# Layer norm of a graph network moved strip by strip into a chain of pooling layers, with the plain pooling as the chain's fifth layer

## The chip, the core and the metric

The kernel runs on one core of one Trainium2 chip. The metric is the device time of one launch in microseconds (us), the median of several runs.

## What is computed

Four small graph networks run one after the other over 6250 nodes with 128 features and 100000 edges; each ends in a residual `x = x + ...`. The change touches the seam between the second and the third:

```python
h = jnp.maximum(_layernorm(x), 0.0)
for l in range(4):                       # second network
    agg = segment_sum(h[src], dst) / max(deg, 1)
    h = h @ W_self[l] + agg @ W_neigh[l] + bias[l]      # then relu, but not after the last
x = x + h
h = jnp.maximum(_layernorm(x), 0.0)      # mean and variance over the 128 features of a node
aggregated = segment_sum(h[src], dst)    # third network: plain pooling, then small products
```

## The kernel before

Nodes lie as 49 blocks of 128 columns in three big tiles with features on the partitions: `A` holds x, `H` holds h, `B` the pooled sums. `C` holds the row of 1/degree, later the pooled edge features. A pooling is a dense product: TensorE multiplies the scaled rows of h (`hs`, 16 bit, two parts "high" and "low" that add up to full precision, nodes on partitions) with a table of edge counts in 8 bit that streams from memory.

`layer_chain` runs such poolings back to back. A **strip** is 7 blocks of nodes (896 columns, two halves in two accumulator banks). Six strips per layer are dense; the seventh (`LAST_S`) is gathered: POOL fetches rows of `hrows` by index in 21 units of 6 indirect DMAs, DVE builds one-hot matrices (L2298), PE multiplies 12 times per unit (L2183). A dense strip is 14 **pieces** of the table, with 16 and 12 matmuls in turn (L2159, 128x448); five pieces are in flight in `tbuf`, and SP loads the next when the oldest is used (L2105, L2106). Everything is written by hand, engine by engine; the pieces' numbers set where side work stands in PE's order:
- after piece 2 of a strip, `turn` makes the next layer's rows from the strip that has just ended: 7 products with the next layer's weight into banks 4 and 5 (L2215); ACT copies the high part out (L2258), DVE the low part (L2310), SP stores the rows to `hrows` (L2110). The gathered strip is turned after piece 12 of strip 5.
- after piece 12, `own_term` multiplies with the layer's own weight (L2195).
- at a strip's end DVE scales the sums out of the banks (L2333 `acc_read`), adds the own term (L2338), and ACT writes `H` (L2267). PE's next strip uses the same two banks and waits for `acc_read` (L2154).

Program order at the seam (`network`): `layer_chain` "sage" with four layers; then `layer_norm` (L921) over all of `A`, in transposed form, where averages over partitions are products with `avg` (L954), `gather` (L960) and `spread` (L976), and which also loads the pooled edge features into `C` (L939) and sets one row of it (L944); then `split_rows` (L1286 transposes `H`, L1272 and L1262 write `hs`, L1220 stores it, L1247 loads the first table pieces); then `layer_chain` "plain" with one layer, whose sums leave the banks by one scaling (L2331). Each of the four is a block of its own: all engines finish before the next begins. `update_nodes` follows.

## Time and profile before

| | us |
|---|---|
| three runs | 3234.71, 3235.70, 3237.24 |
| profiled execution, span | 3240.8 |
| "sage" chain, PE | 1209.98 to 2245.18 |
| seam: layer norm and `split_rows` | 2245.18 to 2304.58 |
| "plain" chain | 2304.58 to 2546.70 |

The span of the profiled execution, 3240.8 us, is the time that is known of it; it is 5.1 us over the median. TensorE is busy for 91% of it, VectorE for 32%, ScalarE for 23%, GpSimd for 34%. A timeline row gives the start, the length, the engine (PEld is PE's weight load, SPq a DMA issue of SP), the line, the operation with what it writes and reads, the number of instructions that were merged, and in brackets the engine's idle time before it and what ended that.

### The profile page before, as it was taken

Reading aid. Unit: us, or ns where it says so; the run is one execution under the profiler, and the core shown is the slowest. Engines: PE = TensorE matmul, PEld = TensorE weight load, DVE = VectorE, ACT = ScalarE, POOL = GpSimd, SP = SyncE. Lnnn points to the kernel's source line nnn. Section 1 sums busy time; section 2 is a strip of 40 time slices with the busy share of each in tenths; the row PEclk is TensorE's granted clock in tenths of the full one; section 3 lists DMA queues with packets and bytes.
Section 4 is the critical chain, followed back from the end, with each engine's and each line's share of the span. In section 5 each row is a group of like instructions: output and inputs, shape, how many; then the busy total and the mean of one; then the engine's idle time right before and its main releaser. Section 6 shows DMA issues by size and latency. Waiting matters only on the chain. (4 is left out here: it accounts for less than half of the span.)

```text
span 3240.8 us, 44117 instructions
## 1 busy us (share of the span) xinstructions
PE 2943.5 (91%) x18657; PEld 1740.9 (54%) x18657; DVE 1047.2 (32%) x1860; ACT 729.8 (23%) x1173; POOL 1114.7 (34%) x1012
## 2 busy tenths in 40 slices
PE   1799969997899869999999999999899877999998
PEld 1688835553444335555555555554355664555554
DVE  5899922223200261211111111113311483222122
ACT  4799912223100230000000000001100383011000
POOL 5000013330000004562562663664167101553564
PEclk6899979998999979999999999999899987999999
DMA  7133599994466226666665665664566213665665
GB/s 260 50 129 129 163 244 173 164 170 89 120 147 146 44 66 206 178 171 169 177 175 165 182 178 163 173 173 121 146 181 179 78 54 101 176 180 161 171 170 156
DMA packets 768367, 492.61 MB, mean 152 GB/s; under 512 B 362500, under 2 KB 749836, under 8 KB 767568
## 3 DMA queue, kind: packets, MB, share of 16 engines
q1 hardware_dynamic: 705362, 395.76, 50.5%
q0 software_dynamic: 30112, 62.69, 6.6%
q10 hardware_dynamic: 32702, 31.44, 3.1%
q8 instruction: 140, 2.29, 0.3%
q14 instruction: 51, 0.42, 0.0%
HBM read 334.89 MB, written 76.82 MB: 127 GB/s over the span
## 5 line engine op out<-in xcount | busy, mean ns | idle before, releaser
L2159 PE MATMUL acc<-tbuf,hs 128*128 128x448 fp8e4 x8232 | 1602.0, 354 | 20.0 <-PEq L1242 8.8
L2136 POOL DMA_INDIRECT grow<-hrows,glist x882 | 940.6, 1066 | 791.9 <-PE acc L2183 388.3
L2159 PEld LDWEIGHTS acc<-tbuf,hs 128*128 128x128 f16 x8232 | 801.2, 98 | 762.9 <-issue 52.5
L2298 DVE TENSOR_TENSOR edge_loc<-iota,gdl 128x768 f16<-128x768 bf16 x147 | 140.6, 971 | 743.9 <-PE acc L2183 714.4
L731 PE MATMUL quad<-K,S 128*128 128x196 bf16 x1568 | 278.0, 250 | 17.6 <-DVE K L655 17.6
L1627 PE MATMUL acc<-tbuf,hs 128*128 128x512 fp8e4 (+1 forms) x1300 | 279.6, 369 | 14.9 <-DMA tbuf<-table 14.9
L711 ACT ACTIVATE stage<-quad 128x784 fp8e4<-128x784 f32 x392 | 287.4, 838 | 11.6 <-PE quad L731 5.8
L735 PE MATMUL deg<-K,S 128*128 128x196 bf16 x1568 | 276.8, 248 | 0.0
L1500 PE MATMUL acc<-tbuf,hs 128*128 128x512 fp8e4 (+1 forms) x1300 | 267.4, 369 | 0.7 <-issue 0.7
L2267 ACT ACTIVATE H<-B,vectors 128x448 f32<-128x448 f32 (+2 forms) x56 | 37.4, 668 | 820.3 <-DVE B L2338 820.3
L1500 PEld LDWEIGHTS acc<-tbuf,hs 128*128 128x128 f16 x1300 | 123.6, 98 | 144.4 <-issue 4.3
L1627 PEld LDWEIGHTS acc<-tbuf,hs 128*128 128x128 f16 x1300 | 119.9, 98 | 139.5 <-issue 17.7
L655 DVE TENSOR_TENSOR K<-iota,win_key 128x2744 bf16<-128x2744 bf16 x112 | 177.1, 1581 | 0.0
L2333 DVE SCALAR_TENSOR_TENSOR B<-acc,scales,C 128x448 f32<-128x448 f32 (+1 forms) x84 | 57.2, 681 | 366.4 <-PE acc L2159 268.7
L731 PEld LDWEIGHTS quad<-K,S 128*128 128x128 bf16 x1568 | 152.2, 97 | 40.5 <-DVE K L655 40.2
L735 PEld LDWEIGHTS deg<-K,S 128*128 128x128 bf16 x1568 | 154.4, 98 | 0.2
L1083 POOL DMA_INDIRECT glist<-edge_pairs,gof x7 | 7.0, 1000 | 357.9 <-SPq L1067 356.0
L1645 DVE TENSOR_TENSOR Z<-iota,edge_loc 128x1024 bf16<-128x1024 bf16 x98 | 73.6, 770 | 170.2 <-PE acc L1609 123.0
L655 DVE TENSOR_TENSOR S<-iota,win_low 128x1792 bf16<-128x1792 bf16 x112 | 122.0, 1089 | 13.6 <-PEq L271 3.5
L2183 PEld LDWEIGHTS acc<-edge_loc,grow 128*128 128x128 f16 x1764 | 110.9, 98 | 24.5
L2183 PE MATMUL acc<-edge_loc,grow 128*128 128x128 f16 x1764 | 122.5, 219 | 0.0
L2125 POOL MEMSET grow<- 128x3072 f16 x3 | 8.0, 2660 | 317.3 <-POOLq L2457 163.7
(301 smaller groups left out, 2008.5 us busy)
## 6 DMA issues: line engine op xcount, KB each, us to landing
tbuf<-table SPq DMA_DIRECT2D x294, 448.0 KB, 3.6
tbuf<-table SPq DMA_DIRECT2D x294, 336.0 KB, 3.2
table<-stage SPq DMA_DIRECT2D x6, 5488.0 KB, 19.4
grow<-hrows,glist POOLq DMA_INDIRECT x882
hrows<-hs SPq DMA_DIRECT2D x28, 448.0 KB, 4.4
feat<-in_edge_attr_dram ACTq DMA_DIRECT2D x27, 448.0 KB, 6.6
C<-factors ACTq DMA_DIRECT2D x2, 3136.0 KB, 12.5
table<-stage SPq DMA_DIRECT2D x2, 2744.0 KB, 12.2
```

The source lines that it names most:

```text
L655: return V.tensor_tensor(to.rearrange("p n (c t) -> p n c t", t=2), iota.rearrange("p (c t) -> p c t", t=2).unsqueeze(1).to_broadcast([P, ...
L711: A.activation(stage[:, b, :, to:to + 4 * WD].rearrange("p b (w d) -> p w b d", d=WD), pair[(h * NQUAD + q) % 3][:, :].rearrange("p (t c) ...
L731: mm = T.matmul(pair[quad % 3][:, at:at + NKEY], S[:, q, i, :], K[:, q, i, :], start=(w % 2 == 0), stop=True, skip_group_check=True)
L735: mm = T.matmul(deg[:, w % 2 * NKEY:(w % 2 + 1) * NKEY], S[:, q, i, :], K[:, q, i, :], start=(w == 0), stop=(u == NHALF * NBATCH - 1 and i ...
L1500: mm = nc.tensor.matmul(acc[h][:, 0:n * P], k.hs[:, j, part, :], counts[:, :, j // 2, :, j % 2], start=(j == 0 and part == 0), stop=(j == ...
L1627: mm = T.matmul(acc[g % 2][:, 0:n * P], k.hs[:, j, part, :], counts[:, :, j // 2, :, j % 2], start=(j == 0 and part == 0), stop=(j == NL - ...
L1645: V.tensor_tensor(Z[:, u % 2, :, :].rearrange("p n (c t) -> p n c t", t=2), k.iota[:, 0:EWIN].rearrange("p (c t) -> p c t", t=2).unsqueeze ...
L2136: g.indirect_dma_start(out=grow[:, n % 2, t, :], out_offset=None, in_=k.hrows[l % 2], in_offset=bass.IndirectOffsetOnAxis(k.glist[:, i // ...
L2159: mm = T.matmul(acc(s, h), rows[l % 2][:, g * US + r, part, :], counts[:, (r - lo) * STRIP + h * HALF:(r - lo) * STRIP + (h + 1) * HALF], ...
L2183: mm = T.matmul(to, grow[:, n % 2, t, part * P:(part + 1) * P], hot[:, n % 2, t, :], start=(not conv and i % GU == 0 and t == 0 and part = ...
L2298: V.tensor_tensor(hot[:, n % 2, :, :], k.iota[:, 0:P].unsqueeze(1).to_broadcast([P, GH, P]), k.gdl[:, i // GU, i % GU * GH:(i % GU + 1) * ...
L2333: V.scalar_tensor_tensor(dst[:, at], acc(s, q), scale(1, l), k.C[:, at], ALU.mult, ALU.mult).then_inc(acc_read.h, 1)
```

## The change

- The chain "sage" gets a fifth layer (`l == LO`), the plain pooling, with scale 0 and neither weight nor own term. `layer_norm`, `split_rows` and the chain "plain" are no longer called there.
- In the fourth layer (`norm`), DVE adds each finished strip plus its bias to `A` (`residual`) where ACT wrote `H`. After piece 2 of the next strip PE transposes the 7 blocks of `A` into banks 4 and 5 (`turn`); DVE takes mean and variance per block there (`moments`), ACT the root, DVE the reciprocal; ACT scales, shifts and clips the 7 blocks into `ny` (`spread`) and writes the high parts, DVE the low parts (`rests`). After piece 8 PE transposes `ny` back (`turn_back`), and ACT copies that to `H` (`back`). The gathered strip is turned after piece 12 of strip 5 and goes back after piece 2 of the fifth layer; strip 5 is turned after piece 3 there.
- The row stores of that layer stand five pieces later in SP's order. The load of `C` stands between table pieces in strip 1 of the fifth layer, the row of ones ahead of that layer's gathers on POOL.
- In every chain PE's wait ahead of a layer's first piece is for strip 4's low parts, no longer for the gathered strip's.

```diff
+BACK_AT, NORM_STORE = 8, 7
...
-    L = len(layers)
+    LO = len(layers)
+    sage, conv = kind == "sage", kind == "conv"
+    L = LO + 1 if sage else LO
     R = k.ring
     total, turns = L * DENSE * NH, (L - 1) * NU
-    sage, conv = kind == "sage", kind == "conv"
+    norm = LO - 1 if sage else None
...
-        return k.scales[:, part, at_scale + l:at_scale + l + 1]
+        at = at_scale + l if l < LO else 0
+        return k.scales[:, part, at:at + 1]
...
+        if sage:
+            ny = k.rstd[:, :, :].rearrange("p a c -> p (a c)")
...
-                        stores[piece + R + 2] = (l, s)
+                        stores[piece + R + (NORM_STORE if l == norm else 2)] = (l, s)
                 for n in range(R, total):
                     sp.wait_ge(used.h, used.at(n - R + 1))
                     load_piece(k, sp, tbuf, n // NH % DENSE, n % NH, n % R)
...
                         l, s = stores[n]
                         sp.wait_ge(z_lo.h, z_lo.at(2 * turned[l, s] + 2))
                         store_rows(k, sp, rows[(l + 1) % 2], (l + 1) % 2, s * US, (s + 1) * US)
+                    if sage and n == LO * DENSE * NH + 2 * NH:
+                        sp.wait_ge(acc_read.h, acc_read.at(count(norm, DENSE - 1, 1)))
+                        sp.dma_start(edges[0:3 * DE, :], k.ea_sums[0:3 * DE, ELEFT:ELEFT + NP]
+                                     ).then_inc(k.sem("easum_in").h, 16)
...
+                    if l == LO:
+                        pool.wait_ge(acc_read.h, acc_read.at(count(norm, DENSE - 1, 1)))
+                        g.memset(edges[3 * DE:3 * DE + 1, :], 1.0)
...
-                        if leaves and j > turns:
+                        if l == norm and normed(l, s):
+                            pe.wait_ge(n_H.h, n_H.at(2 * (normed(l, s) - 1) + q + 1))
+                        elif leaves and j > turns:
...
+                            elif l == norm:
+                                mm = T.transpose(to, k.A[:, b * P:(b + 1) * P], k.idf[:, :])
...
+                def turn_back(l, s):
+                    for q in range(2):
+                        pe.wait_ge(n_y.h, n_y.at(2 * normed(l, s) + q + 1))
+                        for i, b in enumerate(blocks_of(s, q)):
+                            mm = T.transpose(k.bank[4 + q][:, i * P:(i + 1) * P],
+                                             ny[:, (HALVES[q][0] + i) * P:(HALVES[q][0] + i + 1) * P], k.idf[:, :])
+                        mm.then_inc(n_back.h, 1)
...
-                                pe.wait_ge(z_lo.h, z_lo.at(2 * (turned[l - 1, DENSE - 1] - 1) + 2))
+                                pe.wait_ge(z_lo.h, z_lo.at(2 * (turned[l - 1, DENSE - 1] - 2) + 2))
...
-                            if i == TURN_AT:
+                            if i == TURN_AT and sage and l == LO and s == 0:
+                                turn_back(norm, LAST_S)
+                            if i == (TURN_AT + 1 if sage and l == LO and s == 0 else TURN_AT):
                                 for e in events(l, s)[0:1]:
                                     if e[1] != LAST_S:
                                         turn(*e)
-                            if i == OWN_AT and sage:
+                            if i == BACK_AT and events(l, s) and events(l, s)[0][0] == norm:
+                                turn_back(*events(l, s)[0])
+                            if i == OWN_AT and sage and l < LO:
...
+                def spread(l, s):
+                    n = normed(l, s)
+                    act.wait_ge(n_mv.h, n_mv.at(n + 1))
+                    A.activation(nrs[:, :], nmv[:, :, 1], ACT.Sqrt, bias=k.eps[:, 0:1]).then_inc(n_std.h, 1)
+                    act.wait_ge(n_rs.h, n_rs.at(n + 1))
+                    for q in range(2):
+                        lo, hi = HALVES[q]
+                        for i in range(lo, hi):
+                            ins = A.activation(ny[:, i * P:(i + 1) * P], k.bank[4 + q][:, (i - lo) * P:(i - lo + 1) * P],
+                                               ACT.Relu, scale=nrs[:, i:i + 1], bias=nsh[:, i:i + 1])
+                        ins.then_inc(n_y.h, 1)
+                    for q in range(2):
+                        lo, hi = HALVES[q]
+                        act.wait_ge(n_y.h, n_y.at(2 * n + q + 1))
+                        A.activation(rows[(l + 1) % 2][:, s * US + lo:s * US + hi, 0, :],
+                                     ny[:, lo * P:hi * P].rearrange("p (a f) -> p a f", f=P), ACT.Copy,
+                                     scale=scale(0, l + 1)).then_inc(z_hi.h, 1)
+                def back(l, s):
+                    for q in range(2):
+                        b = blocks_of(s, q)
+                        act.wait_ge(n_back.h, n_back.at(2 * normed(l, s) + q + 1))
+                        A.activation(v[:, b[0] * P:(b[-1] + 1) * P], turn_bank(q, len(b)), ACT.Copy).then_inc(n_H.h, 1)
...
-                    if sage:
+                    if sage and l < norm:
...
+                        if sage and l == LO and s == 0:
+                            back(norm, LAST_S)
...
+                def residual(l, s, q):
+                    at = chunk_of(s, q)
+                    dve.wait_ge(moved.h, moved.at(count(l, s, q)))
+                    V.scalar_tensor_tensor(k.A[:, at], dst[:, at], layers[l][3], k.A[:, at], ALU.add, ALU.add
+                                           ).then_inc(ready.h, 1)
+                def moments(l, s):
+                    for q in range(2):
+                        lo, hi = HALVES[q]
+                        dve.wait_ge(z_full.h, z_full.at(2 * turned[l, s] + q + 1))
+                        for i in range(lo, hi):
+                            ins = V.bn_stats(nst[:, i, :], k.bank[4 + q][:, (i - lo) * P:(i - lo + 1) * P])
+                    link(ins)
+                    for i in range(US):
+                        ins = V.bn_aggr(nmv[:, i, :], nst[:, i, :])
+                    ins.then_inc(n_mv.h, 1)
+                    dve.wait_ge(n_std.h, n_std.at(normed(l, s) + 1))
+                    link(V.reciprocal(nrs[:, :], nrs[:, :]))
+                    V.scalar_tensor_tensor(nsh[:, :], nmv[:, :, 0], -1.0, nrs[:, :], ALU.mult, ALU.mult
+                                           ).then_inc(n_rs.h, 1)
+                def rests(l, s):
+                    j = turned[l, s]
+                    for q in range(2):
+                        lo, hi = HALVES[q]
+                        to = rows[(l + 1) % 2][:, s * US + lo:s * US + hi, :, :]
+                        dve.wait_ge(z_hi.h, z_hi.at(2 * j + q + 1))
+                        V.scalar_tensor_tensor(to[:, :, 1, :], ny[:, lo * P:hi * P].rearrange("p (a f) -> p a f", f=P),
+                                               scale(0, l + 1), to[:, :, 0, :], ALU.mult, ALU.subtract
+                                               ).then_inc(z_lo.h, 1)
...
-                    if not sage and not conv:
+                    if not conv and l >= LO - (0 if sage else 1):
...
+                        mine = units(s)[2:] + units(s + 1)[:2]
+                        if sage and l == LO and s == 0:
+                            rests(norm, LAST_S)
                         for e in events(l, s)[0:1]:
-                            if e[1] != LAST_S:
+                            if e[0] == norm:
+                                moments(*e)
+                                for h in mine[:1]:
+                                    hots(l, h)
+                                mine = mine[1:]
+                                rests(*e)
+                            else:
                                 turned_in(*e)
-                        for h in units(s)[2:] + units(s + 1)[:2]:
+                        for h in mine:
                             hots(l, h)
                         parts = [(s, 0), (s, 1)]
+                            if l == norm:
+                                residual(l, LAST_S, 0)
...
                         if s == DENSE - 1:
                             leave_bank(l, LAST_S, 1)
                             if conv:
                                 finish(l, LAST_S, 1)
-                            turned_in(l, LAST_S)
+                            if l == norm:
+                                residual(l, LAST_S, 1)
+                                moments(l, LAST_S)
+                            else:
+                                turned_in(l, LAST_S)
                         for c in parts:
                             leave_bank(l, *c)
+                        for c in parts if l == norm else ():
+                            residual(l, *c)
...
-        k.rstd = sb("rstd", [NCH, 2, CH], F32)
+        k.rstd = sb("rstd", [P, 2, CH], F32)
...
-                layer_chain(k, "sage", H, B, layers, 2, tbuf, factor=1)
+                layer_chain(k, "sage", H, B, layers, 2, tbuf, factor=1, edges=C)
...
-        layer_norm(k, A, H, B, add=True, edges=C)
-        with table_buffer(k, True) as tbuf:
-            split_rows(k, H, True, 0, None, None, tbuf, False, not spilled)
-            if spilled:
+        if spilled:
+            layer_norm(k, A, H, B, add=True, edges=C)
+            with table_buffer(k, True) as tbuf:
+                split_rows(k, H, True, 0, None, None, tbuf, False)
                 pool_neighbours(k, B, None, None, tbuf, False, H, None, 0)
-            else:
-                layer_chain(k, "plain", H, B, [()], 0, tbuf)
```

TensorE at the seam, before (L960 and L976 are the layer norm's averages, L1286 the 49 transposes of `H`, L2159 the plain chain's dense products, L2183 its first gathered unit):

```order
L954 MATMUL acc<-A,avg 128x448
L960 MATMUL acc<-B,gather 7x448 x8
L976 MATMUL acc<-parts,spread 128x448 x14
L935 UNCONDITIONAL_BRANCH
L1276 UNCONDITIONAL_BRANCH
L1286 MATMUL acc<-idf,H 128x128 x49
L1242 UNCONDITIONAL_BRANCH
L2140 UNCONDITIONAL_BRANCH
L2159 MATMUL acc<-tbuf,hs 128x448 x224
L2183 MATMUL acc<-edge_loc,grow 128x128 x12
```

TensorE there now (L2180 dense, L2204 gathered, L2216 own terms, L2238 `turn`, L2248 `turn_back`; the fourth layer ends 12 matmuls into the row of 56):

```order
L2204 MATMUL acc<-edge_loc,grow 128x128 x12
L2216 MATMUL acc<-H,weights 128x384
L2180 MATMUL acc<-tbuf,hs 128x448 x28
L2216 MATMUL acc<-H,weights 128x448 x2
L2238 MATMUL acc<-idf,A 128x128 x7
L2180 MATMUL acc<-tbuf,hs 128x448 x56
L2248 MATMUL acc<-idf,rstd 128x128 x7
L2180 MATMUL acc<-tbuf,hs 128x448 x12
L2238 MATMUL acc<-idf,A 128x128 x7
L2180 MATMUL acc<-tbuf,hs 128x448 x72
L2248 MATMUL acc<-idf,rstd 128x128 x7
L2180 MATMUL acc<-tbuf,hs 128x448 x96
```

The averages are gone, and the transposes stand in groups of 7 between dense products, with no branch to another block. The other five pairs of groups stand in the fourth layer's strips 1 to 5.

VectorE at the end of the fourth layer, before:

```order
L2298 TENSOR_TENSOR edge_loc<-iota,gdl 128x768 x2
L2333 SCALAR_TENSOR_TENSOR B<-acc,scales,C 128x384
L2338 TENSOR_TENSOR B<-B,acc 128x384
L2333 SCALAR_TENSOR_TENSOR B<-acc,scales,C 128x448
L2338 TENSOR_TENSOR B<-B,acc 128x448
L2333 SCALAR_TENSOR_TENSOR B<-acc,scales,C 128x448
L2338 TENSOR_TENSOR B<-B,acc 128x448
L2095 UNCONDITIONAL_BRANCH
```

and now (L2444 and L2449 are the two operations that were L2333 and L2338; L2383 is `residual`, L2409 `rests`):

```order
L2444 SCALAR_TENSOR_TENSOR B<-acc,scales,C 128x384
L2449 TENSOR_TENSOR B<-B,acc 128x384
L2383 SCALAR_TENSOR_TENSOR A<-B,vectors,A 128x384
L2392 BN_STATS nst<-acc 128x6 x7
L2395 BN_AGGR nmv<-nst 128x2 x7
L2398 RECIPROCAL nrs<-nrs 128x7
L2399 SCALAR_TENSOR_TENSOR nsh<-nmv,nrs 128x7
L2444 SCALAR_TENSOR_TENSOR B<-acc,scales,C 128x448
L2449 TENSOR_TENSOR B<-B,acc 128x448
```

The moments of the gathered strip now stand ahead of the operation that frees the first bank for the fifth layer.

SP's queue around the load of `C`, before and now:

```order
L1175 DMA tbuf<-table 128x3x448
L2095 UNCONDITIONAL_BRANCH
L937 UNCONDITIONAL_BRANCH
L939 DMA C<-ea_sums 96x6272
L935 UNCONDITIONAL_BRANCH
```

```order
L1175 DMA tbuf<-table 128x3x448
L1175 DMA tbuf<-table 128x4x448
L2127 DMA C<-ea_sums 96x6272
L1175 DMA tbuf<-table 128x3x448
L1175 DMA tbuf<-table 128x4x448
```

It moved from the idle seam to a place between two table pieces.

## Rows read from the trace of the kernel before

**Rows 1.** Page: busy time and share of the span, by engine.
```profile
PE 2943.5 (91%) x18657; PEld 1740.9 (54%) x18657; DVE 1047.2 (32%) x1860; ACT 729.8 (23%) x1173; POOL 1114.7 (34%) x1012
```

**Rows 2.** Timeline: PE at the end of the chain "sage" (us: start, length).
```profile
2242.75 2.43 PE L2159 MATMUL acc<-tbuf,hs 128*128 128x448 fp8e4 x12
```

**Rows 3.** Timeline: the start of the chain "plain", and DVE at its strip 0's end.
```profile
2304.58 45.35 PE L2159 MATMUL acc<-tbuf,hs 128*128 128x448 fp8e4 x224 [5.74 <-PEq L1242]
...
2343.54 0.68 DVE L2331 TENSOR_SCALAR B<-acc,scales 128x448 f32<-128x448 f32 x1 [37.04 <-PE acc L2159]
```

**Rows 4.** Windows: stretch, busy time by engine, PE's granted clock, DMA share, GB/s.
```profile
2245.18:2304.58 59.40, 40.35 (x120) 14.86 (x120) 42.68 (x66) 20.68 (x35) 5.32 (x1) 0.85 0.43 115
...
2305.00:2315.00 10.00, 10.00 (x41) 4.57 (x40) 1.50 (x2) 0.00 (x0) 5.96 (x5) 0.73 0.52 144
```

**Rows 5.** Chain that ended last, second network after: pieces (start, us, what).
```profile
3020.74 3.03 PE acc L2159 x16
3023.77 0.77 PE acc L2213 x7
3024.53 5.30 PE acc L2159 x28
3029.83 0.67 PE acc L2183 x12
```

**Rows 6.** Timeline: "sage" layer 1, PE and DVE at the ends of strip 5 and strip 0.
```profile
1474.38 8.08 PEld L2159 LDWEIGHTS acc<-tbuf,hs 128*128 128x128 f16 x44 [0.24 <-issue]
...
1482.74 1.73 PE L2215 MATMUL acc<-weights,H 128*128 128x128 f32 x14
...
1510.78 1.67 PE L2195 MATMUL acc<-H,weights 128*128 128x448 f32 x4
...
1513.62 0.68 DVE L2333 SCALAR_TENSOR_TENSOR B<-acc,scales,C 128x448 f32<-128x448 f32 x1 [26.06 <-PE acc L2159]
```

**Rows 7.** Timeline of `update_nodes`: statistics on DVE, then scaling on ACT.
```profile
2552.58 0.86 DVE L2660 BATCH_NORM_STATS2 st_u<-u 128x6 f32<-128x128 f32 x4
...
2558.59 1.65 ACT L2563 ACTIVATE u<-u,sh_u,rs_u 128x128 f32<-128x128 f32 x4 [3.91 <-DVE sh_u L2682]
```

**Rows 8.** Single lines of `update_nodes`: count, duration ns min/median/max.
```profile
L2665 DVE BATCH_NORM_AGGREGATE mv_u<-st_u x196: 147/149/184, 2553.5 to 2701.0; 128x2 f32<-128x6 f32 x196
...
L2571 ACT ACTIVATE rs_u<-mv_u,eps x19: 296/299/308, 2553.9 to 2708.7; 128x16 f32<-128x16 f32 x19
```

**Rows 9.** Waits of PE in "sage": who waited for whom, us, times, longest.
```profile
PE acc L2159 <- DVE B L2333: 6.9, 4, 1.7
...
PE acc L2159 <- DMA tbuf<-table: 2.5, 1, 2.5
```

**Rows 10.** Timeline: a 3136 KB load on ACT's queue beside the table pieces, strip 0.
```profile
1225.48 0.42 ACTq L2275 DMA_DIRECT2D C<-factors  x1
...
1238.51 0.13 PEld L2159 LDWEIGHTS acc<-tbuf,hs 128*128 128x128 f16 x2 [2.91 <-DMA tbuf<-table]
...
1241.85 8.67 PEld L2159 LDWEIGHTS acc<-tbuf,hs 128*128 128x128 f16 x46 [0.22 <-issue]
```

**Rows 11.** DMA issues: size and us to landing; alone, then in 2651:2668, usual.
```profile
C<-ea_sums SPq DMA_DIRECT2D x1, 2352.0 KB, 13.2
...
C<-factors SPq DMA_DIRECT2D x1, 3136.0 KB, 11.3
hrows<-hs SPq DMA_DIRECT2D x1, 1024.0 KB, 14.0
...
tbuf<-table SPq DMA_DIRECT2D x294, 336.0 KB, 3.2
```

**Rows 12.** Timeline: last row store for layer 1, and its first gathers.
```profile
1490.20 0.49 SPq L1220 DMA_DIRECT2D hrows<-hs  x1
...
1494.71 0.99 POOL L2136 DMA_INDIRECT grow<-hrows,glist  x1 [40.33 <-DMA hrows<-hs]
1496.01 1.00 POOL L2136 DMA_INDIRECT grow<-hrows,glist  x1 [0.30 <-issue]
```

27 lines of the change are left out of this document (22 added, 5 removed).

## The prediction

> **What bounds the kernel now.** I read the page first. TensorE is busy for 91% of the span and VectorE for 32% [rows 1], so what counts is where PE doesn't pool. Then I read the timeline at the two chains' borders: PE's last dense product of "sage" ends at 2242.75 + 2.43 = 2245.18 [rows 2], its first of "plain" starts at 2304.58 [rows 3]. The seam between them lasts 59.4 us, in which PE is "busy" for 40 us [rows 4], but with averages and transposes that wait for DVE and ACT: nothing of it is pooling. In a chain, PE is filled with dense products and has hardly any waits: 6.9 us for the banks and 2.5 us for the table in all four layers [rows 9]. So a stage that is hidden there costs only its own instructions on PE.
>
> **What is removed.** The whole seam: -59.4 us on PE's path. With it goes the slow start of "plain". Its strip 0 needs 2343.54 - 2304.58 = 39.0 us until DVE may leave the first bank [rows 3]. The same stretch in layer 1 of "sage" needs 1513.62 - 1474.38 = 39.2 us, of which one turn (1.6) and the own terms (1.5) fall away in a plain layer [rows 6]: 36.1. The difference is 2.8 us, and the window from 2305 shows why, a clock at 0.73 for 10 us, between the levels of 1.2 and 2.4 GHz, 2.7 us lost [rows 4]. If PE never stops, this is saved too: -2.8. The rest of the plain layer, 241 us, stays as it is.
>
> **What is added on PE.** 14 groups of 7 transposes (7 strips, there and back). A group of 7 transposes of this kind, in the midst of dense products, takes 0.77 us on the chain of waits, where 16 dense matmuls take 3.03 and 28 take 5.30 [rows 5]. 14 x 0.77 = +10.8. I take it for exact; if half the groups cost as much as a turn with weights (1.6 us [rows 6]), it would be 16.6, the upper bound.
>
> **Does the norm of a strip hide?** From the end of a turn, T: statistics of 7 blocks at 0.215 each (0.86 for 4 [rows 7]) 1.5, which start while the turn ends, so T+1.4; 7 aggregates at 0.147, 1.0; root 0.30 [rows 8]; reciprocal and product on as small tiles, taken at the root's price, 0.6; for four hand-overs I add 0.4. That gives T+3.7. ACT's 7 blocks at 1.65 / 4 = 0.41 [rows 7] take 2.9: `ny` is full at T+6.6. High and low parts, two operations on each engine of 0.6 to 0.7 us, end at about T+9. PE comes to `turn_back` after 6 pieces in strips 1 to 5 (84 matmuls, 15.9 us) and after 5 in the last (13.6 us). It needs the last strip's rows at piece 10, 14.4 us after that turn. The cover is 14 against 7, and 14 against 9: no wait. The statistics here read the banks and not SBUF, which no row shows; even at double their price they end 2.5 us later and stay hidden. Without that cover each microsecond beyond it would be paid 7 times.
>
> **One place where it doesn't hide.** The gathered strip is turned after piece 12 of strip 5, and its moments stand on DVE ahead of the operation that frees bank 0. The queue behind the wait for ACT's root is DVE's own: `leave_bank` (5,0), and behind that PE, which wants the bank for the fifth layer one piece after T, at T+2.3 (12 matmuls). DVE gets to it at T+3.7 and needs 0.68 [rows 6]: T+4.4. Stall: +2.0, once; bounds 1.3 and 3.0. Two waits of 1.7 us for the same banks are known from before [rows 9]. The low parts' wait ahead of a layer's first piece, which now is looser, costs nothing before (PE goes on after 0.24 us [rows 6]); 0.
>
> **The later row stores.** They stand five pieces later, and the fifth layer's gathers wait for the last one. From that layer's start: 10 pieces 26.5, three groups 2.3, SP's issue 0.6: 29.4. From issue to the first gather 4.5 us [rows 12], then six gathers 1.3 apart [rows 12]: the last ends at 41.4. PE wants the first unit after 16 pieces, 224 matmuls 42.4 + 2.3 = 44.7. Three us are left for the last gather to land, which no row shows by itself. +0.5, bounds 0 and 2. The row of ones (a POOL instruction of 5.3 us [rows 4]) ends long before and is hidden by the same wait.
>
> **The load of `C`.** This is the DMA that was moved, from an idle seam to a busy queue. Alone it lands after 13.2 us [rows 11]. Behind it on SP's queue stand table pieces, of which PE has 5 in hand: 72 matmuls and one gathered unit, 14.3 us. Does a piece behind it wait? In `update_nodes` a row store that is issued 0.4 us after a 3136 KB load on this same queue lands after 14.0 us, 3 us after the load is through [rows 11]. So yes. At that store's pace (1024 KB in 3 us) the piece ahead of the load takes 1.3 us; the piece behind it 1.0 by that pace, or its usual 3.2. It lands at 13.2 + 1.3 + 1.0 to 3.2 = 15.5 to 17.7, and PE waits 1.2 to 3.4 us. The other case is the load of 3136 KB on ACT's queue beside the pieces: PE waited 2.5 us [rows 9, 10]. Both meet at +2.5, which I take; bounds 0 (gaps in the load used by the pieces) and 6 (the gathers take a share as well). After that earlier wait PE's weight loads of 0.15 us stand with 0.22 us between them, 0.37 us for each, instead of 0.19, from 1238.5 to 1241.85 [rows 10]: the clock's lower level, for 9 matmuls, 1.7 us. After waits of 1.7 us no such row follows. I add +1.7 for this stall, and nothing for the one of 2.0.
> Trainium skill, page "DMA: Bandwidth & Descriptors", section "Queues, rings and completion order": on each DMA engine the descriptors of one ring are taken in order, and the engine goes round between the queues that have work. This speaks against the new place: by the rule, pieces of another queue would share with the load, and those behind it in SP's ring can't. The trace agrees with the first part in the pieces beside ACT's load, and with the second in the store of 14.0 us; the rule alone would put the stall at the upper end, 3.4, 0.9 us above my value.
>
> **Sum.** -59.4 - 2.8 + 10.8 + 2.0 + 0.5 + 2.5 + 1.7 = -44.7. The profiled execution becomes 3240.8 - 44.7 = 3196.1. It stood 5.1 us above the median of 3235.7; taken off the median, **3191.0 us**.
>
> **Rivals.**
> 1. *The load of `C` hides after all* and the clock stays up: -4.2, so 3186.8. For it: the DMA engines are only half busy at such a place [rows 4]. Against it: the store of 14.0 us. 20%.
> 2. *The norm's chain is longer than its cover, or the small operations get in the way of others* (one-hot matrices that DVE builds late for gathers, statistics from the banks): 2 us in each of the 7 strips is +14, 3205.0. For it: DVE's order has three new places where it waits. Against it: 14 us of cover for 7 to 9 us of work. 13%.
> 3. *The chain doesn't close*: at the border PE waits for something that I have not seen, and half of the seam comes back as idle time (30 us): 3221.0. For it: five engines' queues, each in strict order, must fit together. Against it: the order shows dense products on both sides of the border, and the waits point to work that is long done. 3%.
> 4. *Slower than before.* The place is `turn_back`: PE stands in its strict order in front of it until ACT has filled `ny`. If a strip's norm took x us, each strip would cost x - 15.9 us (13.6 in the last). It decides from (44.7 / 7) + 15.6 = 22 us per strip; at 24 us the kernel would need 3191.0 + 7 x 8.4 = 3249.8. The rows for the parts add up to a third of that, so 2%.
> 5. *The sum is too careful*: no stall at all, neither for the bank, the gather or the table: -51.4, so 3184.3. 7%.
>
> **How the numbers follow.** The forecast's own case, all terms within their bounds, 3187 to 3199, holds 55%. Rivals 1 and 5 below it and most of rival 2 above are taken in with 3184 to 3206. The bounds' ends together (transposes 16.6, bank 3.0, gather 2, load 6 and two falls of the clock 3.4) give -31.2, 3204.5; the lower ends (1.3, 0, 0) give -50.1, 3185.6. What the range leaves out, rivals 3 and 4, part of rival 2 and mishaps outside all cases, is 10 to 15%. A measurement of this kernel can tell 0.2%, 6.5 us, from no change; nearly all cases are far below that. Faster 0.95, same 0.02, slower 0.03.
>
> **What will show it.** The fourth layer's last dense product and the fifth's first should be 2 us apart, with the wait on DVE's `B`, not 59. A group of 7 transposes should add 0.8 us. DVE's `BATCH_NORM` rows should take 0.2 to 0.3 us and ACT's root follow within 4 us of a turn; `turn_back` should show no wait. One wait of PE for `tbuf` should stand in strip 2 of the fifth layer, 2 to 3 us long, with weight loads 0.37 us apart behind it; none there means rival 1. A wait of PE for `grow` in strip 1 of that layer speaks on the gather term. Waits before transposes in every strip would mean rival 2 or 4. The prediction fails as a whole if the time around the seam was not PE's alone, so that work after it (`update_nodes`, the last chain) becomes longer in turn.

## The result, and the profile after

| | before | changed |
|---|---|---|
| median, us | 3236.5 (3234.7 to 3244.9) | **3194.2** (3187.7 to 3200.5) |
| ratio | 1 | 0.9869, 95% interval 0.9855 to 0.9883 |
| the same two kernels measured again | 3236.6 (3233.6 to 3242.1) | 3190.7 (3189.0 to 3192.7); ratio 0.9859 (0.9844 to 0.9874) |
| span of the profiled execution | 3240.8 | 3192.1 |

The change brings 42 us in the first comparison and 46 in the second. The forecast was 44.7 less, 3191.0 us. The two traces lie 48.7 us apart; the table below shows which part of that belongs to the change.

The page of the changed kernel, busy time by engine. It answers to [rows 1]: TensorE is busy 33 us less, and still for 91% of the span.

```profile
PE 2910.6 (91%) x18636; PEld 1733.9 (54%) x18636; DVE 1040.9 (33%) x1937; ACT 737.7 (23%) x1210; POOL 1108.2 (35%) x1011
```

The timeline of PE around the old seam: start and length in us, line, operation, count, and in brackets the idle time ahead of it with what ended it. L2238 is the turn there, L2248 the turn back.

```profile
2246.79 0.93 PE L2238 MATMUL acc<-idf,A 128*128 128x128 f32 x7
2247.55 2.43 PE L2180 MATMUL acc<-tbuf,hs 128*128 128x448 fp8e4 x12
2251.04 8.48 PE L2180 MATMUL acc<-tbuf,hs 128*128 128x448 fp8e4 x44 [1.05 <-DVE B L2444]
2259.36 0.93 PE L2248 MATMUL acc<-idf,rstd 128*128 128x128 f32 x7
2260.12 2.43 PE L2180 MATMUL acc<-tbuf,hs 128*128 128x448 fp8e4 x12
2262.39 0.93 PE L2238 MATMUL acc<-idf,A 128*128 128x128 f32 x7
2263.16 13.78 PE L2180 MATMUL acc<-tbuf,hs 128*128 128x448 fp8e4 x72
2276.78 0.93 PE L2248 MATMUL acc<-idf,rstd 128*128 128x128 f32 x7
2277.54 18.32 PE L2180 MATMUL acc<-tbuf,hs 128*128 128x448 fp8e4 x96
```

Where 59.4 us lay between two dense products [rows 2, 3], one wait of 1.05 us is left. The 12 products ahead of it are the fourth layer's last piece; the fifth layer begins with the 44 behind it. The dense products go on 0.76 to 0.77 us after the start of each group of transposes, and no group waits.

What VectorE and ScalarE do in the same stretch, one strip's norm:

```profile
2247.43 1.49 DVE L2392 BATCH_NORM_STATS2 nst<-acc 128x6 f32<-128x128 f32 x7 [5.96 <-PE acc L2238]
2248.95 0.58 DVE L2395 BATCH_NORM_AGGREGATE nmv<-nst 128x2 f32<-128x6 f32 x7
2249.56 0.30 ACT L2293 ACTIVATE nrs<-nmv,eps 128x7 f32<-128x7 f32 x1 [15.38 <-DVE nmv L2395]
2249.89 0.20 DVE L2398 RECIPROCAL nrs<-nrs 128x7 f32<-128x7 f32 x1 [0.37 <-ACT nrs L2293]
2250.13 0.17 DVE L2399 SCALAR_TENSOR_TENSOR nsh<-nmv,nrs 128x7 f32<-128x7 f32 x1
2250.21 0.68 DVE L2444 SCALAR_TENSOR_TENSOR B<-acc,scales,C 128x448 f32<-128x448 f32 x1
2250.33 2.55 ACT L2298 ACTIVATE rstd<-acc,nsh,nrs 128x128 f32<-128x128 f32 x7 [0.47 <-DVE nsh L2399]
...
2253.90 1.27 DVE L2409 SCALAR_TENSOR_TENSOR hs<-rstd,scales,hs 128x512 f16<-128x512 f32 x2
```

The waits of PE in the chain of five layers (whole time, how often, the longest); they answer to [rows 9]:

```profile
PE acc L2180 <- DVE B L2444: 8.0, 5, 1.7
PE acc L2180 <- DMA tbuf<-table: 7.3, 2, 4.4
```

One more wait for a bank (the 1.05), and a second one for a table slot: the 4.4 us, at the place of the load of `C`. The issue on SP's queue, PE's first dense product behind the wait, and its weight loads at the lower clock, 0.37 us apart:

```profile
2319.50 0.50 SPq L2127 DMA_DIRECT2D C<-ea_sums  x1
2322.12 19.88 SPq L1175 DMA_DIRECT2D tbuf<-table  x6
...
2337.77 3.82 PE L2180 MATMUL acc<-tbuf,hs 128*128 128x448 fp8e4 x12 [4.42 <-DMA tbuf<-table]
...
2338.12 0.15 PEld L2180 LDWEIGHTS acc<-tbuf,hs 128*128 128x128 f16 x1 [0.22 <-issue]
2338.49 0.15 PEld L2180 LDWEIGHTS acc<-tbuf,hs 128*128 128x128 f16 x1 [0.22 <-issue]
```

The DMA issues of 2319 to 2342 (KB, us to landing); [rows 11] had 13.2 for the same load alone:

```profile
C<-ea_sums SPq DMA_DIRECT2D x1, 2352.0 KB, 16.1
```

**Where the time went.** I cut both traces at three places of PE: the first dense product of the chain, its first gathered unit, and the first product of `update_nodes`.

| us | before | changed | difference |
|---|---|---|---|
| up to the first dense product | 1210.0 | 1209.4 | -0.6 |
| to the first gathered unit | 49.9 | 46.9 | -3.0 |
| to `update_nodes` (**"the stretch"** from here on) | 1287.2 | 1242.7 | **-44.5** |
| to the end | 693.8 | 693.2 | -0.6 |

The -3.0 belong to no edit. They are the clock of the first 128 dense products, 24.37 us at the upper level and 26.06 where it starts late, and of the 56 behind the first layer's wait (10.77 or up to 12.45), less 0.4 for that wait's own length. Over the kernels below whose first layer is the same, that stage lies between 46.9 and 50.1 us and follows this clock and the length of that wait (2.48 to 3.65 us): before 49.9, e6 (before's chain) 48.9, e1 and e5 (the changed chain) 50.0 and 50.1. The last row moves without an edit too: the changed kernel traced a second time (e8) has 690.2 us there, and all thirteen traces lie between 690.0 and 694.0. So the stretch, in which the unchanged kernel repeats to 0.1 us, is what I compare below.

### The profile page after: what moved, and what is told of

Its sections match the earlier page's. It is cut to its first block and busy times, and to the rows that moved or that the text cites. A ratio compares the mean times of both kernels' runs of the same rounds, so it can differ in the third digit from the quotient of the medians.

```text
span 3192.1 us, 44150 instructions
## 1 busy us (share of the span) xinstructions
PE 2910.6 (91%) x18636; PEld 1733.9 (54%) x18636; DVE 1040.9 (33%) x1937; ACT 737.7 (23%) x1210; POOL 1108.2 (35%) x1011
## 5 line engine op out<-in xcount | busy, mean ns | idle before, releaser
L2180 PE MATMUL acc<-tbuf,hs 128*128 128x448 fp8e4 x8232 | 1599.5, 353 | 20.0 <-DVE B L2444 8.0
L2180 PEld LDWEIGHTS acc<-tbuf,hs 128*128 128x128 f16 x8232 | 799.7, 98 | 757.7 <-issue 42.2
L731 PE MATMUL quad<-K,S 128*128 128x196 bf16 x1568 | 277.7, 250 | 15.9 <-DVE K L655 12.5
L2444 DVE SCALAR_TENSOR_TENSOR B<-acc,scales,C 128x448 f32<-128x448 f32 (+1 forms) x84 | 57.2, 681 | 357.3 <-PE acc L2180 259.9
L2336 ACT ACTIVATE H<-B,vectors 128x448 f32<-128x448 f32 (+2 forms) x42 | 28.1, 668 | 584.3 <-DVE B L2449 584.3
L2204 PEld LDWEIGHTS acc<-edge_loc,grow 128*128 128x128 f16 x1764 | 110.9, 98 | 24.4
L2204 PE MATMUL acc<-edge_loc,grow 128*128 128x128 f16 x1764 | 122.5, 219 | 0.0
L2339 ACT ACTIVATE B<-B,vectors 128x448 f32<-128x448 f32 (+2 forms) x28 | 18.7, 668 | 421.9 <-DVE H L2452 421.7
```

The lines of the kernel that those rows point to most:

```text
L731: mm = T.matmul(pair[quad % 3][:, at:at + NKEY], S[:, q, i, :], K[:, q, i, :], start=(w % 2 == 0), stop=True, skip_group_check=True)
L2180: mm = T.matmul(acc(s, h), rows[l % 2][:, g * US + r, part, :], counts[:, (r - lo) * STRIP + h * HALF:(r - lo) * STRIP + (h + 1) * HALF], ...
L2204: mm = T.matmul(to, grow[:, n % 2, t, part * P:(part + 1) * P], hot[:, n % 2, t, :], start=(not conv and i % GU == 0 and t == 0 and part = ...
L2444: V.scalar_tensor_tensor(dst[:, at], acc(s, q), scale(1, l), k.C[:, at], ALU.mult, ALU.mult).then_inc(acc_read.h, 1)
```

## The experiments

Unless something else is said, each is the changed kernel with one edit. e1 to e6, e9 and e10 are one launch each, the traced one, so their total times say little beside a difference of a few microseconds; what counts is the stretch. "Stage" in the recorded texts is mostly the time from the chain's first dense product, that is the stretch and the first layer's 46.9 to 50.1 us with its changing clock; I judge them by the stretch.

### What does the load of `C` cost, and why?

Theory: pieces behind it on SP's queue have to wait for their turn. Rival: it is the amount of data at once. **e1** has it on ACT's queue.

```diff
-if sage and n == LO * DENSE * NH + 2 * NH:                     # SP
-    sp.wait_ge(acc_read.h, ...); sp.dma_start(edges[0:3 * DE, :], ...)
+if sage and l == LO and s == 1:                                # ACT
+    act.wait_ge(used.h, used.at(LO * DENSE * NH + 2 * NH - R + 1))
+    act.wait_ge(acc_read.h, ...); act.dma_start(edges[0:3 * DE, :], ...)
```

> The same 2352 KB load of C at the same moment, but issued on ACT's queue instead of SP's. In the changed kernel PE waits 4.4 us for a table piece there, and 1.4 us more go to the lower clock behind it. Theory (order in the queue): pieces no longer stand behind the load, so the wait falls to 0 to 2.5 us (the 3136 KB load on ACT's queue costs 2.5 to 2.8 us in the first layer), and PE's time from the first dense product of the chain to the first product of update_nodes falls by 2 to 5.8 us. Rival (bandwidth alone: the DMA engines have the same bytes to move): the wait stays at 4 us, the stage is unchanged within 1 us.

Measured: 3197.6 us; the stretch 1245.2, 2.6 longer. The wait did not go, it grew, and came one piece earlier; neither the theory nor the rival had it longer. Timeline of PE, and the DMA queues in the midst of the load, in 2326:2334 (packets, MB, share of the 16 engines; q10 is ACT's, q1 SP's):

```profile
2340.23 7.34 PE L2176 MATMUL acc<-tbuf,hs 128*128 128x448 fp8e4 x28 [6.51 <-DMA tbuf<-table]
```
```profile
q10 hardware_dynamic: 69, 1.73, 96.7%
q1 hardware_dynamic: 70, 0.06, 4.1%
```

The load moves 69 packets of 25 KB there, one per row, and the table 70 of 0.9 KB: one for one. So the load has 96.7% of the engines' time and the pieces 4.1%, the pieces that were ahead of it on SP's queue among them. The Trainium skill, page "DMA: Bandwidth & Descriptors", section "Queues, rings and completion order", says that an engine changes queues at packet granularity, taking a whole packet from one ring before the next. The trace agrees with these counts; I had used the rule without asking for the size of a turn.

In the changed kernel, with the load on SP's queue, the same stretch of the load (2323:2332) reads:

```profile
DMA packets 131, 2.13 MB, mean 236 GB/s; under 512 B 20, under 2 KB 20, under 8 KB 51
q1 hardware_dynamic: 79, 1.98, 98.5%
```

The 79 packets of SP's queue hold 25 KB each on average, rows of the load, and none in the whole stretch has the size of the table's 0.9 KB (as many are under 2 KB as under 512 B): for 9 us the pieces behind the load get nothing. So the order within the queue is how the wait comes about there, as the theory had it. What e1 refutes is that leaving this queue helps: sharing packet by packet with rows of 25 KB left the pieces hardly more than nothing, and the wait began one piece earlier.

**e5** cuts the load into seven parts of 896 columns on SP's queue, one every 7 pieces, and `update_nodes` waits for all seven.

```diff
-if sage and n == LO * DENSE * NH + 2 * NH:
-    sp.dma_start(edges[0:3 * DE, :], k.ea_sums[0:3 * DE, ELEFT:ELEFT + NP]).then_inc(...)
+part = n - LO * DENSE * NH - 2 * NH
+if sage and part >= 0 and part % 7 == 0 and part // 7 < EDGE_PARTS:
+    at = part // 7 * STRIP
+    sp.dma_start(edges[0:3 * DE, at:at + STRIP],
+                 k.ea_sums[0:3 * DE, ELEFT + at:ELEFT + at + STRIP]).then_inc(...)
```

> The load of C stays on SP's queue, in 7 parts of 336 KB (896 columns each), one behind every seventh table piece from the same place on. Theory (a piece behind the load waits for the whole load): a part delays the pieces by some 2 us, less than the 14 us that PE has in hand, so PE waits for no piece and the clock stays up: stage -5.8 us against the changed kernel. Rival (the bytes beside the table stream are what costs): the 4.4 us come back in small waits, stage unchanged within 1 us.

Measured: 3189.2 us; the stretch 1236.7, 6.0 shorter, as the theory said. PE has no wait for the table in the fifth layer. The parts, in 2310:2490:

```profile
C<-ea_sums SPq DMA_DIRECT2D x7, 336.0 KB, 4.8
```

So the load costs 5.8 to 6.0 us in the changed kernel: 4.42 of wait, and 1.4 because 12 products took 3.82 us instead of 2.43.

Parts differ from the one load in two ways: pieces go between them, and their rows are short. **e9** issues all seven at once on SP's queue, **e10** all seven at once on ACT's.

```diff
 if sage and n == LO * DENSE * NH + 2 * NH:                     # e9: SP; e10: at e1's place, ACT
-    sp.dma_start(edges[0:3 * DE, :], ...)
+    for at in range(0, NP, STRIP):
+        sp.dma_start(edges[0:3 * DE, at:at + STRIP], ...)
```

> The changed kernel, with the load of C cut into the seven parts of 896 columns as in e5, but all seven issued one behind the other at the place of the one load, on SP's queue. It tells the length of a row (12.5 KB of padded columns before, 3.5 KB now) from the amount that is ahead of the table's next piece. Theory A (what counts on this queue is the 2352 KB ahead of the next piece; the parts of e5 helped because the pieces went between them): PE's wait for a table slot in strip 2 of the fifth layer stays, 3.5 to 5 us, and the stretch from the first gathered unit to update_nodes stays at 1242 to 1244 us. Theory B (long rows move badly, short ones don't): the wait falls below 1 us and the stretch is 1236 to 1238 us, as in e5.

> The same seven parts, all issued one behind the other at the same moment on ACT's queue. e1 had the one load there: the wait was 6.5 us and one piece earlier, against 4.4 on SP's queue. Theory C (the two queues take turns packet by packet, so the load's 22 KB packets take most of the engines' time against the table's of under 2 KB): with packets of 3.5 KB the table keeps a third or more of the engines' time, about 90 of the 180 GB/s that PE uses; over the 14 us of the load it falls some 7 us of work behind, which the full slots nearly cover (the 13.4 us of work that e0's load displaces became a wait of 4.4, so they cover about 9). Expected wait 0 to 1.5 us, stretch 1236 to 1239 us. Theory D (the amount at once decides, whatever the row): wait 4.4 to 6.5 us, stretch 1242 to 1246 us.

("e0's load" in the second text is the one of the changed kernel. The first text gives a row of the one load as 12.5 KB; it is 24.5 KB, 2352 KB over 96 rows.) Measured: e9 3190.0 us, e10 3195.9. The wait in each, and the queues of e10 in 2334:2338:

```profile
2335.61 3.84 PE L2183 MATMUL acc<-tbuf,hs 128*128 128x448 fp8e4 x12 [2.93 <-DMA tbuf<-table]
```
```profile
2342.52 3.95 PE L2177 MATMUL acc<-tbuf,hs 128*128 128x448 fp8e4 x12 [4.27 <-DMA tbuf<-table]
```
```profile
q10 hardware_dynamic: 216, 0.67, 62.2%
q1 hardware_dynamic: 215, 0.19, 21.0%
```

| 2352 KB | SP's queue: wait, stretch | ACT's queue: wait, stretch |
|---|---|---|
| at once, long rows | 4.42, 1242.7 | 6.51, 1245.2 |
| at once, seven parts | 2.93, 1241.5 | 4.27, 1242.7 |
| spread over 42 pieces | none, 1236.7 | not run |

The one load was traced at its place in five kernels, with waits of 4.3 to 4.7 us, so the differences in the table are clear of that. My theory C for e10 (0 to 1.5 us) fell, and so did B for e9 (below 1 us): short rows take 2.2 us off the wait on ACT's queue and 1.5 on SP's, but the amount at once keeps the larger part. A (3.5 to 5 us) and D (4.4 to 6.5) were nearer, and both a little too high. In this part of e10 the queues again move packets one for one (216 and 215), with 3.1 KB in one of the load's on average: it has 62.2% of the time, and the table 21.0%, not the third that C wanted. On SP's queue there are no such turns, and part of the gain must be another: by the rows of 2323:2332 the long rows take 98.5% of 9 us for 1.98 MB, and e9's short ones in 2323:2331 86.0% of 8 us for 1.73 MB:

```profile
q1 hardware_dynamic: 564, 1.73, 86.0%
```

That is an estimate of 10.8 us of all engines for the whole load in long rows and 9.6 in short ones, 1.2 of the 1.5 us. No run takes the two effects apart on ACT's queue.

The windows of the changed kernel compare the load with what the engines have left (stretch, busy time by engine, clock, DMA share, GB/s):

```profile
2265.00:2300.00 35.00, 35.00 (x199) 18.82 (x197) 5.83 (x11) 4.94 (x12) 11.16 (x11) 1.00 0.68 188
...
2319.00:2330.00 11.00, 11.00 (x69) 5.95 (x66) 1.64 (x2) 0.00 (x0) 8.52 (x9) 1.00 1.00 244
2330.00:2340.00 10.00, 5.58 (x25) 2.46 (x24) 0.68 (x1) 0.00 (x0) 2.00 (x2) 0.86 0.99 268
```

The layer itself uses 188 GB/s at a DMA share of 0.68; with the load the engines are full at 244 to 268. That leaves 56 to 80 GB/s, and 2.41 MB in 16 us want 150. Whatever the order, PE's pieces lose the rest, which at 188 GB/s is 6 to 8 us of work; the full slots cover a part of it, and 4.4 are seen. In e5 the parts are issued over 119 us, so that the load wants 20 GB/s, and each lands after 4.8 us, less than the 14 us of pieces that PE has in hand. The budget is an account from these rows; what the runs show is that spreading cures the wait and that neither another queue nor short rows alone does.

### Does DVE's place for the moments cost the bank wait?

**e2** puts the moments of the gathered strip behind the operations that free the banks.

```diff
 if l == norm:
     residual(l, LAST_S, 1)
-    moments(l, LAST_S)
 ...
 for c in parts:
     leave_bank(l, *c)
+if l == norm and s == DENSE - 1:
+    moments(l, LAST_S)
```

> The moments of the gathered strip stand behind the operations that free the two banks on DVE, not ahead of them. Theory: PE's wait of 1.05 us ahead of the fifth layer's first product goes (0 to 0.2 us), and the norm of that strip, some 3 us later, is still covered by the pieces ahead of turn_back: stage -1.0 us. Rival: what PE waits for there is something else that ends at the same time, or turn_back now waits as long: stage unchanged.

Measured: 3188.2 us; the stretch 1241.7, 0.9 shorter, as the theory had it. In PE's timeline dense product follows dense product, and the turn back 10.6 us later still waits for nothing:

```profile
2244.04 0.93 PE L2238 MATMUL acc<-idf,A 128*128 128x128 f32 x7
2244.81 10.76 PE L2180 MATMUL acc<-tbuf,hs 128*128 128x448 fp8e4 x56
2255.40 0.93 PE L2248 MATMUL acc<-idf,rstd 128*128 128x128 f32 x7
```

### What is the looser wait for the low parts worth?

In the changed kernel PE waits ahead of a layer's first piece for one strip fewer than before. I had put that at 0. **e3** takes the wait back to what it was.

```diff
-... turned[l - 1, DENSE - 1] - 2) + 2
+... turned[l - 1, DENSE - 1] - 1) + 2
```

> PE's wait ahead of a layer's first piece is for the gathered strip's low parts again, as in the kernel before. Theory: in the fifth layer these end at T+7.6 after the strip's turn, 5.4 us after PE gets there, so the wait grows from 1.05 to 5.4 us and the clock falls behind it: stage +4.3 to +6.0 us; at the starts of layers 2, 3 and 4 nothing changes (0.2 us at most). Rival: other waits come anyway within those 5 us (turn_back, the bank), so that it costs less than 2 us.

Measured: 3200.3 us; the stretch 1250.2, 7.5 longer, above the range of the text. Timeline of PE at the border:

```profile
2256.67 10.86 PE L2180 MATMUL acc<-tbuf,hs 128*128 128x448 fp8e4 x44 [5.25 <-DVE hs L2409]
```

The wait costs 4.2 more than the one of 1.05; behind it 44 products take 10.86 us instead of 8.48 (2.4). These 6.6 us lie at the border. The other 0.9 lie at the load of `C` (a wait 0.25 longer, products behind it 0.7), where traces without this edit differ by 0.3 (e2, e8), so that it is not shown whether they belong to it. Layers 2 to 4 start as before, without a new wait. So the edit is worth nothing where it stood, and 6.6 to 7.5 us once the norm's chain ends at the border.

### How long may a strip's norm be?

**e4** gives ACT four passes instead of one over each strip's 7 blocks, 7.7 us more per strip.

```diff
+for r in range(3):                                             # pad is ny
+    for q in range(2):
+        lo, hi = HALVES[q]
+        for i in range(lo, hi):
+            ins = A.activation(pad[:, i * P:(i + 1) * P], k.bank[4 + q][...], ACT.Relu, scale=nrs[...], bias=nsh[...])
+    ...                                                        # ACT waits for its own pass
 for q in range(2):                                             # the pass that counts, as before
```

> ACT scales and clips the 7 blocks of a strip four times instead of once, the first three for nothing, one after the other: each strip's norm is 7.8 us longer. Theory (cover of 13.6 to 15.9 us per strip, of which 5.3 are used): only the gathered strip's turn_back (11.8 us after its turn, n_y now at 13.1) and the last strip's rows (needed 14.4 us after the turn, there after 15) become late: +1 to +4 us in all. Rival (each microsecond of a strip's norm counts in every strip): +30 to +55 us.

Measured: 3191.2 us; the stretch 1245.0, 2.3 longer. Timeline of ACT and PE (L2181 is the dense product there, L2249 the turn back):

```profile
2247.40 7.73 ACT L2300 ACTIVATE rstd<-acc,nsh,nrs 128x128 f32<-128x128 f32 x21 [0.47 <-DVE nsh L2408]
...
2257.77 0.55 PE L2249 MATMUL acc<-idf,rstd 128*128 128x128 f32 x3 [0.39 <-ACT rstd L2307]
2258.15 2.43 PE L2181 MATMUL acc<-tbuf,hs 128*128 128x448 fp8e4 x12
...
2274.81 0.93 PE L2249 MATMUL acc<-idf,rstd 128*128 128x128 f32 x7
```

54 us more of ACT's work cost PE 1 us, all at the gathered strip, whose cover is the shortest (11.8 us). The other 1.4 lie at the load of `C`: its wait is 4.72 instead of 4.42, and the 12 products and the gathered unit behind it take 1.1 longer. The edit doesn't touch that place, and it is not shown why. The last strip's rows, which the text expected late too, cost no wait. The other six strips hide 13 us of norm (5.3 + 7.7 until `ny` is full) whole. So the length of a strip's norm, on which rivals 2 and 4 rest, was far from costing anything.

### Is the slow start of "plain" the clock?

**e6** is the kernel *before*, with 42 products into an unused bank at the end of the seam, whose results nobody reads.

```diff
+if store and weight is None:
+    for _ in range(42):
+        nc.tensor.matmul(k.bank[6][:, 0:2 * P], k.idb[:, :], k.iota[:, 0:2 * P], start=True, stop=True)
```

> The kernel before with 42 products of 128x256 into an unused bank at the end of split_rows ahead of the chain plain, whose results nobody reads: PE is busy while SP's stores finish, instead of idle for 5.7 us. Theory (the plain chain starts at the lower clock because PE was idle): strip 0 of that chain, from its first product to DVE's first operation on the bank, takes 36.2 us instead of 39.0, the granted clock in its first 10 us is near 1.0 instead of 0.73, and the stage is 2.8 us shorter. Rival (the slow start is the table's first pieces or the start of the block): it stays at 38 to 39 us. The seam is not shortened in either case; if the products outlast the stores it is longer by up to 1 us.

Measured: 3234.6 us; the stretch 1284.3, 2.9 shorter than before's.

```profile
2296.09 4.75 PE L1292 MATMUL acc<-iota,idb 128*128 128x256 bf16 x42
2302.25 42.53 PE L2162 MATMUL acc<-tbuf,hs 128*128 128x448 fp8e4 x224 [1.41 <-PEq L1242]
...
2338.39 0.68 DVE L2334 TENSOR_SCALAR B<-acc,scales 128x448 f32<-128x448 f32 x1 [34.22 <-PE acc L2162]
```
```profile
2300.00:2310.00 10.00, 8.59 (x49) 4.54 (x48) 1.83 (x2) 0.00 (x0) 5.38 (x4) 1.00 0.77 215
```

From the first product to DVE's operation 2338.39 - 2302.25 = 36.1 us, against 39.0 [rows 3], and a clock of 1.00 where it was 0.73 [rows 4]. The seam is as long as it was (59.3 us against 59.4), so what became shorter is this strip: the term of -2.8 is the clock.

### The pieces together

**e7** is e5 and e2 in one, launched five times.

> The changed kernel with both repairs: C in 7 parts, and the moments of the gathered strip behind the operations that free the banks. Theory: the two waits and the lower clock go, 1.05 + 4.4 + 1.4 = 6.9 us less than the changed kernel, stage 1282.7 us; ratio to the kernel before 0.985. Rival (new waits take their place): stage 1287 or more, ratio as for the changed kernel, 0.987.

Measured: 3185.7 us (3184.7 to 3188.0), ratio to before 0.9844 (0.9831 to 0.9857). The stretch is 1235.5, 7.2 shorter than the changed kernel's; with the first layer it is 1282.5 us, where the text had 1282.7.

**e8** is the changed kernel again, beside e7 on the same chip.

> The changed kernel once more, beside the repaired one on the same chip: ratio to the kernel before 0.9869 within its interval of 0.9855 to 0.9883; stage from the chain's first dense product to update_nodes 1289.6 us, or up to 3 us more where the first layer starts at the lower clock as it does in the kernel before.

Measured: 3190.7 us, ratio 0.9859, the stretch 1242.6, the same as in the first trace. The medians of e7 and e8 lie 5.0 us apart, the stretches of their traces 7.1. The parts and the moments are all that differs; the medians also hold what moves without an edit (up to the first gathered unit and behind the chain).

**e11** adds one edit to e7: the first layer's load of `C<-factors` (3136 KB on ACT's queue, behind which PE waited 2.5 us in before [rows 9]) in seven parts on SP's queue, one every 7 pieces. DVE waits strip by strip for what it needs.

```diff
-act.dma_start(k.C[:, :], k.factors[factor:factor + 1, :].to_broadcast([P, NP])).then_inc(row_in.h, 16)
+if factor is not None and n >= R and (n - R) % 7 == 0 and (n - R) // 7 < EDGE_PARTS:   # SP
+    at = (n - R) // 7 * STRIP
+    sp.dma_start(k.C[:, at:at + STRIP], k.factors[factor:factor + 1, at:at + STRIP]...).then_inc(row_in.h, 16)
-dve.wait_ge(row_in.h, row_in.at(16))
+if factor is not None and l == 0 and s < 4:
+    dve.wait_ge(row_in.h, row_in.at(16 * min(2 * s + 2, EDGE_PARTS)))
```

> e7 (the load of C in parts, the moments behind leave_bank) and besides the first layer's load of C<-factors, 3136 KB in one on ACT's queue, cut into seven parts of 448 KB on SP's queue, one every 7 pieces, with DVE waiting for those it needs strip by strip instead of for all. In e7 PE waited 2.94 us for a table slot behind that load, and the matmuls behind it ran at the lower clock for some microseconds. If the cause is the same as for C: that wait falls to below 0.5 us, the stretch from the first dense product to the first gathered unit goes from 47.0 to 43 to 44 us, the rest stays at 1235.4 and the time is 3181.5 us (3180 to 3184). If the first layer's wait has another cause (the stores of hrows and the gathers that lie in the same stretch): the wait stays over 2 us and the time is 3184 to 3187.

Measured: 3182.2 us (3177.9 to 3187.6), ratio to before 0.9838 (0.9825 to 0.9852). The first 184 dense products stand without a gap:

```profile
1208.36 34.97 PE L2190 MATMUL acc<-tbuf,hs 128*128 128x448 fp8e4 x184 [2.93 <-PEq L1242]
```

From the first dense product to the first gathered unit it is 43.9 us instead of 47.0, and the rest 1235.5 as in e7. The trace shows the 3.1 us; the medians of e7 and e11 lie 3.5 apart, but their ranges overlap, and they were taken on two chips. The edit changes the queue and cuts the load at once, so it doesn't say which of the two helps here. It is the best version that was run: 54 us less than before.

## Why the prediction was right

Its -44.7 is the stretch, which became 44.5 shorter; the medians' differences of 42.3 and 45.9 us lie on both sides of it. Term by term:

| term | predicted | measured | by |
|---|---|---|---|
| seam | -59.4 | -59.4 | nothing of it is left but the waits below |
| slow start of "plain" | -2.8 | -2.8 | e6 |
| 14 groups of transposes | +10.8 | +10.8 | 0.77 between the starts, in every group |
| bank | +2.0 | +1.05 | 0.9 by e2 |
| first gather | +0.5 | 0 | no wait for `grow` |
| load of `C` | +4.2 | +5.8 | 6.0 by e5 |
| sum | -44.7 | -44.55 | |

**The bank.** The mechanism was right (e2), the size was not. DVE was at `leave_bank` 2.7 us after the turn and not 3.7. The aggregates over 7 blocks take 0.58 us from the first's start to the last's end and not 1.0, since I took the 0.147 of a single one in `update_nodes` [rows 8] for the pace, and their records overlap. The four hand-overs are in the rows' gaps, 0.1 to 0.4 us. ACT's seven blocks took 2.55 against 2.9, so `ny` was full 5.3 us after the turn against 6.6: the room under the cover was larger than told, as e4 then showed. No lower clock followed the 1.05, as assumed.

**The first gather.** The last row store was issued at 2280.41 and the first gather began 5.1 us later, not 4.5, yet PE had the first unit without a wait:

```profile
2280.41 0.51 SPq L1220 DMA_DIRECT2D hrows<-hs  x1
...
2285.49 1.00 POOL L2157 DMA_INDIRECT grow<-hrows,glist  x1 [27.97 <-DMA hrows<-hs]
...
2295.70 0.83 PE L2204 MATMUL acc<-edge_loc,grow 128*128 128x128 f16 x12
```

**The load of `C`.** The place and the kind of wait were right, and so was the step "does a piece behind it wait? so yes": for 9 us SP's queue moved nothing but the load. Wrong was what stood beside it, that on another queue the pieces would share and so fare better: they share packet by packet, which left them 4.1% and made the wait 2.1 us longer (e1). By size: the load landed after 16.1 us where I had 13.2 + 1.3, and the cover was 13.85 and not 14.3. Table packets ahead of the load still moved more than 2 us after its issue, and the gathers were at work beside it; no run takes these two apart. It was 18.3 until the piece behind it was there, beyond my upper 17.7, and the wait of 4.4 was beyond my 3.4, though within the bounds of 0 to 6 that I took. The clock's part was 1.4 for 1.7 predicted. Too small here and too large at the bank and the gather: the sum's 0.15 us of error is luck, each term missed by up to 1.6.

**What the sum did not hold** is the looser wait. It was priced at nothing because the same wait cost nothing in the kernel before. For the time predicted that is right, since the edit is in; as a price of the edit it is wrong by 6.6 to 7.5 us (e3). Without it the kernel would have come out that much later, and the change would have looked worse for a reason that no row of before shows.

**The rivals.** 1 and 5 (the load hides) fell with the 4.4 us. 2, 3 and 4 did not occur, and e4 shows how far away 2 and 4 were, as far as they rest on the length of the norm: with 7.7 us more per strip they were still not reached. The tail behind the chain did not grow: it lies between 690.0 and 694.0 us in the eleven traces with a fifth layer, and is 693.8 and 691.1 in the two of the chain before (before and e6). So the seam's time was PE's alone, to within these 4 us.

## What to carry to other kernels

A stage that sits between two chains on the bounding engine costs its whole length; laid strip by strip into the chain it costs only its own instructions there, and how much slack it has is best measured by making it longer on purpose. When a large transfer is moved into a busy stretch, compare what it wants per microsecond with what the engines have left; another queue made it worse here and short rows helped a little, but cutting it and spreading the parts took the wait away. A wait that costs nothing today must be priced again at the place where the change makes another chain end.

## What the hardware showed

- **A gap of 2.4 to 3.7 us on PE ended at the lower clock in some traces and not in others.** Behind the first layer's wait for the table 56 products took 10.77 us in six of the traces (waits of 2.84 to 3.37) and 12.24 to 12.45 in the six others (waits of 2.48 to 3.65), whatever the kernel. Two rows with the same wait:

```profile
1236.59 10.77 PE L2180 MATMUL acc<-tbuf,hs 128*128 128x448 fp8e4 x56 [2.84 <-DMA tbuf<-table]
```
```profile
1238.52 12.24 PE L2176 MATMUL acc<-tbuf,hs 128*128 128x448 fp8e4 x56 [2.84 <-DMA tbuf<-table]
```

  The first is the changed kernel, the second e1. Behind the wait of 1.05 it did not fall (44 products in 8.48 us); behind all eight of 4.3 to 6.5 it did, for 1.4 to 2.5 us, and in e9 behind one of 2.93 as well. What PE did before has a part in it: the chain's first 128 products took 26.06 us in the four traces in which PE had been idle for 3.07 to 3.13 us ahead of them, and 24.37 in the eight with 2.38 to 2.97; those four all fell again behind the wait that followed, of the eight others only two did. So a term such as my +1.7, taken from one wait of 2.5 us, was not certain; it held because the wait became 4.4.
- **Two busy queues moved packets one for one, whatever their sizes; on one queue what stood behind got nothing.** Beside the table's packets of 0.9 KB a load on another queue moved 69 of 25 KB against 70 in 8 us (e1), and 216 of 3.1 KB against 215 in 4 us (e10; in other parts of that load one of the queues moved nearly alone, so the counts hold for these 4 us); PE waited 6.5 and 4.3 us. On the pieces' own queue no table packet moved for 9 us, and PE waited 4.4.
- **Small statistics in a row overlap.** Seven aggregates span 0.58 us (0.083 each), though each is recorded with 0.147 to 0.184, as in `update_nodes` [rows 8]; seven statistics of a 128x128 block from PSUM span 1.49 (0.213 each, as from SBUF [rows 7]), and each is recorded with 0.278 to 0.300. The reciprocal and the product on 128x7 take 0.20 and 0.17.
